# An attention and mixture block: the first LayerNorm by transposes instead of ones-vector sums, the expert gate ahead of the base GEMM, and weights loaded in rows

## The reference

```python
q = (x @ Wq.T).reshape(B, S, 16, 128)      # k, v likewise
scores = einsum('bshd,bsgd->bshg', q, k) / sqrt(128)   # heads of one token attend to each other
out = einsum('bshg,bsgd->bshd', softmax(scores), v).reshape(B, S, 2048)
x1 = layernorm(x + out @ Wo.T)
result = x1 @ base_w.T + base_b
probs = softmax(x1 @ router_w.T + router_b)
top_vals, top_idx = top_k(probs, 2)         # renormalised to a gate [token, 8]
mid = einsum('nd,edr->ner', x1, lora_A) * gate[:, :, None]
y = layernorm(x1 + result + 2.0 * einsum('ner,erd->nd', mid, lora_B))
```

## Time and profile before

| what | value |
|---|---|
| time, median of the runs shown | 2489.07 us (2457.67 and 2520.48) |
| profiled execution, device time | 2460.02 us |
| its span on the slowest core | 2458.4 us (other cores 2449.4 to 2455.0) |
| PE busy | 2221.6 us, 90% of the span |
| DVE, ACT busy | 1190.9 us (48%), 843.7 us (34%) |
| PE's granted clock, mean | 0.965 of full speed |
| HBM read, written | 180.70 MB, 8.39 MB |

### The profile page before, as it was taken

One profiled execution on the slowest core, in us unless ns is written; L12 is line 12 of the kernel. 1 busy time (PEld: TensorE's weight loads), 2 busy tenths in 40 slices (PEclk: granted clock), 3 DMA queues, 4 the chain that ended last, 5 costly groups with the idle time before them and its releaser, 6 DMA issues.

```text
span 2458.4 us, 32440 instructions; the slowest of 8 cores (2449.4 to 2458.4 us)
## 1 busy us (share of the span) xinstructions
PE 2221.6 (90%) x8920; PEld 1563.1 (64%) x8920; DVE 1190.9 (48%) x2085; ACT 843.7 (34%) x1514; POOL 12.6 (1%) x22
## 2 busy tenths in 40 slices
PE   6998999999899998899789999989998999888995
PEld 4666666666776651566566666666668666435664
DVE  2454444454654434544545445444447444255444
ACT  2333333333443420333333333333334343212333
POOL 0000000000000000000000000000000000000000
PEclk9999999999999998899889999999999999988997
DMA  4222222222112220222332222222220222111221
GB/s 138 86 78 78 86 86 86 78 78 86 36 58 82 78 78 7 79 78 82 142 112 84 84 82 79 85 78 86 81 83 19 79 78 80 58 43 61 78 86 78
DMA packets 50060, 191.19 MB, mean 78 GB/s; under 512 B 5632, under 2 KB 6048, under 8 KB 47584
## 3 DMA queue, kind: packets, MB, share of 16 engines
q1 hardware_dynamic: 47680, 176.38, 20.6%
q0 software_dynamic: 2208, 12.73, 1.5%
HBM read 180.70 MB, written 8.39 MB: 77 GB/s over the span
## 4 chain that ended last, share of the span: by engine, by line
PE 85%; DVE 6%; issue 5%; ACT 2%; DMA 1%; DVEq 0%; ACTq 0%; SPq 0%; POOL 0%; POOLq 0%
PE pb L238 29%; PE pb L245 23%; PE pb L254 23%; PE pb L771 1%; PE pb L764 1%; PE pb L678 1%; PE pb L688 1%; PE pb L371 1%; PE pb L423 1%; PE pb L861 1%; DVE xsp L213 1%; ACT xsp L210 1%; PE pb L407 1%; DMA wrawD<-wqT 1%; DVE bufC L328 1%
## 5 line engine op out<-in xcount | busy, mean ns | idle before, releaser
L238 PE MATMUL pb<-xsp,whi 128*128 128x512 f32 x2560 | 757.6, 418 | 137.1 <-DVE xsp L213 77.4
L238 PEld LDWEIGHTS pb<-xsp,whi 128*128 128x128 f32 x2560 | 439.4, 191 | 442.5 <-issue 383.0
L245 PE MATMUL pb<-xsp,whi 128*128 128x512 f32 x2560 | 700.6, 396 | 0.0
L254 PE MATMUL pb<-xsp,wlo 128*128 128x512 f32 x2560 | 694.1, 393 | 0.0
L245 PEld LDWEIGHTS pb<-xsp,whi 128*128 128x128 f32 x2560 | 487.8, 191 | 111.4
L254 PEld LDWEIGHTS pb<-xsp,wlo 128*128 128x128 f32 x2560 | 487.2, 190 | 107.8
L201 ACT CAST whi<-wrawD 128x512 fp32r<-128x512 f32 x320 | 198.4, 620 | 633.8 <-PE pb L254 601.9
L213 DVE TENSOR_TENSOR xsp<-xTs,xsp 128x512 fp32r<-128x512 f32 x384 | 265.5, 692 | 273.6 <-PE pb L245 273.6
L204 DVE TENSOR_TENSOR wlo<-wrawD,whi 128x512 fp32r<-128x512 f32 x320 | 221.3, 692 | 307.5 <-PE pb L238 234.8
L210 ACT CAST xsp<-xTs 128x512 fp32r<-128x512 f32 x384 | 236.7, 616 | 0.0
L201 ACT CAST whi<-bufA 128x512 fp32r<-128x512 f32 x128 | 79.4, 620 | 285.3 <-PE pb L254 285.3
(11 more groups left out here) (113 smaller groups left out, 888.5 us busy)
## 6 DMA issues: line engine op xcount, KB each, us to landing
wrawD<-wqT SPq DMA_DIRECT2D x32, 512.0 KB, 3.4
bufB<-wqT SPq DMA_DIRECT2D x32, 512.0 KB, 3.4
wrawD<-wkT SPq DMA_DIRECT2D x32, 512.0 KB, 3.3
avT<-wkT SPq DMA_DIRECT2D x32, 512.0 KB, 3.3
wrawD<-wvT SPq DMA_DIRECT2D x32, 512.0 KB, 3.2
avT<-wvT SPq DMA_DIRECT2D x32, 512.0 KB, 3.2
wrawD<-woT SPq DMA_DIRECT2D x32, 512.0 KB, 3.2
bufA<-woT SPq DMA_DIRECT2D x32, 512.0 KB, 3.2
```

Source lines behind the costliest of these rows:

```text
L238: e.matmul(pb[b][0:128, 0:T], whiB[wbi][:].bitcast(F32R)[:, j * 128:(j + 1) * 128], xhiB[wbi].bitcast(F32R), start=st, stop=False),
L245: e.matmul(pb[b][0:128, 0:T], whiB[wbi][:].bitcast(F32R)[:, j * 128:(j + 1) * 128], xloB[wbi].bitcast(F32R), start=False, stop=False),
L254: e.matmul(pb[b][0:128, 0:T], wloB[wbi][:].bitcast(F32R)[:, j * 128:(j + 1) * 128], xhiB[wbi].bitcast(F32R), start=False, stop=sp),
```

## The change

The five weights and the input stay plain two-dimensional arrays, and each transfer picks rows out of them: of a weight two runs of 2 KB for each partition, of the input four runs of 2 KB. The squares in the GEMM with Wo go. The first LayerNorm is done by `gen_ln` with its `back` part, in four chunks, with the two halves of `SH` as buffers. Router and lora A are two separate runs of 16 matmuls, and the whole gate stands between them and ahead of the base GEMM; `base_mid` keeps the last two DVE operations and is called at step 2. The small loads of the bias and of lora A wait for the end of the first LayerNorm.

```diff
-    d_wq = nc.dram_tensor("wqT", [D * D], F32, kind="ExternalInput").ap()
+    d_wq = nc.dram_tensor("wqT", [D, D], F32, kind="ExternalInput").ap()
...
                             emit("sync", lambda e, kc=kc, oc0=oc0, pair=pair:
-                                 e.dma_start(out=pair,
-                                             in_=wsrc(kc, oc0, 4)),
+                                 e.dma_start(
+                                     out=pair.rearrange("p (c e) -> p c e", c=2),
+                                     in_=wsrc(kc, oc0, 4, nkc=2)
+                                     .rearrange("(c p) e -> p c e", p=128)),
                                  waits=dw, inc=wsem, by=16)
...
-                        if q == 0 and ki == 8 and mid_cb is not None:
+                        if q == 0 and ki == 2 and mid_cb is not None:
                             mid_cb()
                         if ki == 2 and pending:
                             for fnp in pending:
                                 fnp()
                             pending = []
-                            if flush_cb is not None:
-                                flush_cb(q - 1)
...
-                for kq in range(4):
-                    off = (tile * 4 + kq) * 128 * 4 * T
-                    emit("sync", lambda e, kq=kq, off=off:
+                for kc in range(0, KC, 4):
+                    emit("sync", lambda e, kc=kc:
                          e.dma_start(
...
+                             in_=d_xT[kc * 128:(kc + 4) * 128, t0:t0 + T]
+                             .rearrange("(c p) t -> p c t", p=128)),
+                         waits=([x_free[0]] if kc == 0 else ()), inc="lx", by=16)
...
-                def wo_flush(qq):
-                    for oc in range(qq * 4, qq * 4 + 4):
-                        sq_se[oc] = emit("scalar", lambda e, oc=oc:
-                            e.activation(out=bufB[:, oc * T:(oc + 1) * T],
-                                         in_=xT[:, oc * T:(oc + 1) * T],
-                                         func=AF.Square),
-                            waits=[("dv", wo_ev[oc])], inc="se")
...
-                    lastsx = emit("tensor", lambda e, kc=kc:
-                        e.matmul(pb[0][0:1, 0:T], onesc[:],
-                                 xT[:, kc * T:(kc + 1) * T],
...
-                    sqmm[kc] = emit("tensor", lambda e, kc=kc:
-                        e.matmul(pb[1][0:1, 0:T], onesc[:],
-                                 bufB[:, kc * T:(kc + 1) * T],
...
-                        e.tensor_tensor(bufB[:, kc * T:(kc + 1) * T],
-                                        xT[:, kc * T:(kc + 1) * T],
-                                        pb[3][0:128, 0:T], op=ALU.mult),
...
+                x1n_dv = gen_ln(xT, bufB, src_ready=("dv", x1_dv))
+                x_free[0] = ("pe", cnt["pe"])
...
                 emit("gpsimd", lambda e: e.dma_start(
                      out=laT.rearrange("p (kc r) -> p kc r", r=128),
                      in_=d_la[:].rearrange("(kc p) r -> p kc r", p=128)),
-                     waits=[x1tok_free_g[1], ("dv", x1_dv)],
+                     waits=[x1tok_free_g[1], ("dv", x1n_dv)],
                      inc="la", by=16)
...
+                rw_w = [("lg", rw_ld), ("dv", x1n_dv), bank_free[rbank]]
                 for kc in range(KC):
-                    wr = [("dv", nrmB[kc])]
...
+                for c in range(NCH):
+                    t = GT2[c]
+                    lgt = emit("tensor", lambda e, c=c:
+                        e.matmul(pb[gbank][0:128, 0:8],
+                                 logT2[:, c * 128:(c + 1) * 128], i8[:],
+                                 is_transpose=True, start=True, stop=True),
+                        waits=[("dv", lge), bank_free[gbank]], inc="pe")
+                    lev = emit("vector", lambda e, t=t:
+                               e.tensor_copy(t["lgtok"], pb[gbank][0:128, 0:8]),
+                               waits=[("pe", lgt)], inc="dv")
+                    bank_free[gbank] = ("dv", lev)
...
+                la_w = [("la", la_ld), ("dv", x1n_dv), bank_free[labank]]
+                for kc in range(KC):
+                    lastm = emit("tensor", lambda e, kc=kc:
                         e.matmul(pb[labank][0:128, 0:T],
                                  laT[:, kc * 128:(kc + 1) * 128],
                                  bufB[:, kc * T:(kc + 1) * T],
...
+                    gxt_m[c] = emit("tensor", lambda e, c=c:
+                        e.matmul(pb[gbank][0:128, c * 128:(c + 1) * 128],
+                                 gexp2b[c], i128[:],
...
                 def base_mid():
-                    gate_chains()
...
                     emit("vector", lambda e:
                         e.tensor_copy(gateT2[:, 0:T], pb[gbank][0:128, 0:T]),
                         waits=[("pe", gxt_m[NCH - 1])], inc="dv")
```

More of the change, by code:

```diff
@@ L186, in stream_gemm @@
                         wcount[0] += 1
-                        pair = wrawD[:] if wri < 2 else w2ap
+                        pair = wrawD if wri < 2 else w2ap
                         wsem = wbuf_sem[wri // 2]
@@ L512, in program @@
                             w2ap=bufA[:, 0:1024],
[L513 to L514 removed]
+                            w2wait=[("pe", score1_pe[0])])
                 x1_dv = cnt["dv"]
@@ L671, in program @@
-                emit("vector", lambda e, onesr=onesr: e.memset(onesr, 1.0),
-                     waits=[("dv", x1_dv)], inc="dv")
-                lastsx = None
-                for kc in range(KC):
-                    w = [("dv", x1_dv), bank_free[0]] if kc == 0 else []
-                    lastsx = emit("tensor", lambda e, kc=kc:
-                        e.matmul(pb[0][0:1, 0:T], onesc[:],
-                                 xT[:, kc * T:(kc + 1) * T],
-                                 start=(kc == 0), stop=(kc == KC - 1)),
-                        waits=w, inc="pe")
@@ L682, in program @@
-                sqmm = {}
-                for kc in range(KC):
-                    w2 = [("se", sq_se[kc])]
-                    if kc == 0:
-                        w2.append(bank_free[1])
-                    sqmm[kc] = emit("tensor", lambda e, kc=kc:
-                        e.matmul(pb[1][0:1, 0:T], onesc[:],
-                                 bufB[:, kc * T:(kc + 1) * T],
-                                 start=(kc == 0), stop=(kc == KC - 1)),
-                        waits=w2, inc="pe")
@@ L707, in program @@
-                bank_free[1] = ("dv", var_dv)
-                sd_se = emit("scalar", lambda e:
-                    e.activation(out=rrow, in_=m2row, func=AF.Sqrt,
-                                 scale=1.0, bias=epsv[0:1, 0:1]),
-                    waits=[("dv", var_dv), ("dv", eps_dv)], inc="se")
-                emit("vector", lambda e: e.reciprocal(rrow, rrow),
-                     waits=[("se", sd_se)])
-                emit("vector", lambda e: e.drain())
-                mr_dv = emit("vector", lambda e:
-                    e.tensor_tensor(mrrow, murow, rrow, op=ALU.mult), inc="dv")
@@ L717, in program @@
-                rbc = emit("tensor", lambda e:
-                    e.matmul(pb[3][0:128, 0:T], onesr, rrow,
-                             start=True, stop=True),
-                    waits=[("dv", mr_dv), bank_free[3]], inc="pe")
-                emit("tensor", lambda e:
-                    e.matmul(pb[2][0:128, 0:T], onesr, mrrow,
-                             start=True, stop=True),
-                    waits=[bank_free[2]], inc="pe")
-                bc_pe = cnt["pe"]
-                nrmB = {}
@@ new lines, in program @@
+                bank_free[rbank] = ("dv", lge)
+                for c in range(NCH):
+                    t = GT2[c]
[8 more added lines that the diff above has]
+                    bank_free[gbank] = ("dv", lev)
+                    emit("vector", lambda e: e.drain())
+                    emit("vector", lambda e, t=t: e.reduce_max(t["m1"], t["lgtok"], axis=AX.X))
+                    emit("vector", lambda e: e.drain())
+                    emit("vector", lambda e, t=t: e.tensor_scalar(t["eq1"], t["lgtok"], t["m1"], None, op0=ALU.is_equal))
+                    emit("vector", lambda e: e.drain())
+                    emit("vector", lambda e, t=t: e.scalar_tensor_tensor(t["l2t"], t["eq1"], NEG_BIG, t["lgtok"], op0=ALU.mult, op1=ALU.add))
+                    emit("vector", lambda e: e.drain())
+                    emit("vector", lambda e, t=t: e.reduce_max(t["m2"], t["l2t"], axis=AX.X))
+                    emit("vector", lambda e: e.drain())
+                    g1 = emit("vector", lambda e, t=t: e.tensor_tensor(t["ddt"], t["m2"], t["m1"], op=ALU.subtract), inc="dv")
+                    emit("vector", lambda e, t=t: e.tensor_scalar(t["eq2"], t["lgtok"], t["m2"], None, op0=ALU.is_equal))
+                    ge_m[c] = emit("scalar", lambda e, t=t:
+                                   e.activation(out=t["e2t"], in_=t["ddt"], func=AF.Exp),
```

(11 more changed lines are left out.)

200 lines of the change are left out of this document (55 added, 145 removed).

## The result

The changed kernel takes 2435.9 us (median of 9 runs) beside 2460.8 for the kernel before (8 runs); the ratio of the two is 0.990, 95% interval 0.989 to 0.992. It is 24.9 us or 1.0% faster; 35.5 us had been forecast, and the range holds the time. (In some executions one die runs at a lower clock; these are left out of ratios, and medians are given where they are not touched by it.)

What follows compares the result with a forecast made beforehand. The prediction took PE's GEMM matmuls to bound the kernel. Per tile 3.4 - 13.5 - 8.4 = -18.5 us, two tiles -37.0, start +1.5: -35.5 from 2460.0, that is 2425 us, range 2406 to 2458.

Steps and rivals of the forecast that it cites:

- What bounds the kernel: Whole kernel: PE sets the end; work beside running GEMM steps is free, whatever stops a step or separates GEMMs is paid.
- Gate out of the base GEMM: Base GEMM, steps 7 to 9: moving the gate's small DVE operations out gives -13.5 us a tile, between -12.5 and -14.
- Squares: Wo GEMM, step 2 of quarters: without ACT's squares three flushes save 2.8 us each, -8.4 us a tile.
- Between the GEMMs: Wo GEMM to base GEMM: LayerNorm 44.5, router 15.5, then 0.2 and 20.5, together 80.7 us against 77.3, +3.4 a tile.
- Transfers: Weights and input in 2 KB runs: 0 in the GEMMs, +1.5 us at the start, where nothing covers them.
- the stretch: From the first PE instruction after the last addition into `xT` to the base GEMM: 80.7 us, +3.4 a tile.
- PE was at full clock in the router: Rival between the GEMMs: PE stays at half clock through router and lora A, +31.0 us a tile, 2480 us; chance 0.07.
- no weight was late: Rival in the GEMMs: weights in 2 KB runs land later than the 7.5 us allowed, 2505 us with e = 0.5; chance 0.05.
- the additions alone cost 0.6 a flush: Rival in the Wo GEMM: DVE's additions, not the squares, stop it; only the gate's part comes, 2442 us; chance 0.10.
- no 2% were gained: Rival for the whole: LayerNorm at full clock, no slow starts, a start that gains; 2408 us or a little under; chance 0.12.

Runs made afterwards that it cites:

- e3_gate8: Changed kernel with the gate's chains and transposes put back into the base GEMM at step 8: 2450.2 us, 14.3 above the changed kernel.
- e1_rows: Kernel before with only the changed kernel's row transfers of 2 KB: 2461.8 us, ratio to before 1.0003.
- e4_tiled: Changed kernel with the transfers of the kernel before: 2435.2 us, 0.7 below the changed kernel.
- e5_shift: Kernel before with the memset of `onesc` moved from the start into the first LayerNorm: ratio to before 1.001 (0.998 to 1.004).
- e6_memset: Changed kernel with the memset of `onesc` put back at the start: ratio to before 0.988 (0.981 to 0.995).
- e9_turn_at_once: Changed kernel with old transfers, memset back, router in four parts, lora A's weight loaded after attention, logits' transposes at once: 2397.3 us, ratio to before 0.9743.

## Why the prediction was right, and where it was off

- **What bounds the kernel** held: PE, and what stops it. But for the start and 2.9 us in the attention, the difference lies in steps that something stops and between the GEMMs.
- **Gate out of the base GEMM**, -13.5 a tile: measured -14.0 and -13.2, and +14.0 when it is put back.
- **Squares**, -8.4 a tile: -5.6 and -8.2 in the traces, and 14.0 in both tiles when they are put back. The mechanism was right (the wait on ACT's line 210 is gone); the size was off, since I took one flush for all three. By the steps the three flushes give 2.8, 2.9 and 1.5, which is 7.2 a tile: the 2.11 us wait costs 1.5 each time, the slow step behind it only sometimes. Four late starts of line 213 in the first tile's Wo GEMM take 1.4 of it away; that the second tile comes near the forecast is luck, since its first Wo step is 0.8 shorter (4.43 instead of 5.26), which no flush explains.
- **Between the GEMMs**, 80.7 us: measured 81.8. The parts: LayerNorm 46.2 for 44.5 (the clock was nearer to half than I took it; half gave 47), router 13.9 for 15.5 (its clock was full from its first matmul), lora A 4.9 behind the bias for 4.6, and 16.0 long for 15.4. That the errors of 1.7 and 1.6 in the first two cancel is luck. One sentence of it was wrong: "the gate in front costs nearly nothing, since it lies beside lora A". `e3_gate8` shows that it costs 7 us a tile, because lora A starts 3.6 later, and its first 3.5 us run at clock 0.50. The sum had those numbers in it, the sentence didn't.
- **Transfers**: 0 in the GEMMs and +1.5 at the start; measured 0 and +2.3 on core 0, +1.2 by the medians of the cores. The Trainium skill, "DMA: Bandwidth & Descriptors", Specifications, with line rate from 512 B on, would make it 0; the measurement shows a small cost at the start, where nothing hides it, which `e1_rows` and `e4_tiled` put at 0.9 to 1.0 us.
- **The step that failed** is the one never written down: that stages whose code is untouched keep their time. I had taken "in the GEMMs: 0" from the transfers alone. Against it stand +6.8 us: 4.2 for the 12 longer steps, caused by a memset that is no longer there (`e5_shift`, `e6_memset`), and 2.9 in the two attention stages (60.21 and 60.00 to 61.64 and 61.42), less 0.3 elsewhere. The attention varies from 58.6 to 63.0 us over cores and kernels with the same code, `e1_rows` with 61.94 among them, so core 0 alone says little. By the medians of the cores, though, the first tile's takes 59.3 to 59.7 in the eight profiled executions with the memset at the start and 60.8 to 61.2 in the six without it: there some 1.5 us go with the memset too. The second tile's shows no such split, and its cause stays open.

So -35.5 became -23.7: squares +3.0, the stretch +1.4, the start +0.8, the untouched stages +6.8, the base GEMM -0.2. The +0.8 of the start is particular to core 0. The forecast of 35.5 against a measured 24.9 got the direction, the stages and most of their prices; the range, 2406 to 2458, was so wide that it would have held a gain of 2 us or of 54, and the hit says little. None of the rivals came: PE was at full clock in the router, no weight was late, the additions alone cost 0.6 a flush, and no 2% were gained.

## What to carry to other kernels

Where an engine's wait stops a running GEMM, price the stop from several of its occurrences: the wait itself comes each time, the slow clock behind it only sometimes. A piece of serial work moved out of a GEMM to a place beside a long matmul run still costs what it delays that run's start, so look for what in it is needed first, and give that own columns or banks (as `e9_turn_at_once` does, together with an earlier load). And a change at the start of an engine's stream can move the time of unchanged code by some tenths of a per cent; before explaining a difference of 5 us in 2400, see at which steps it sits.

## What the runs showed of the hardware

- DVE has starts that are late by 0.34 to 0.41 us with no semaphore to blame, 128 records of its stream apart or a multiple of that (128 records are about 48 us of these GEMMs): all waits of PE for such a start, 136 over the eight cores of the changed kernel, fall on records 59 + 128 n, in every kernel here that has any. Whether it costs anything depends on which record stands there; one instruction more at the start of the program moves it. What happens there was not tried.
- A PE wait of 2.11 us was at some flushes followed by matmuls at a lower clock (steps of 4.1 to 4.5 us) and at others not, in the same kernel: in the kernel before the granted clock of the step behind was 0.66, 0.61 and 1.00 at the three flushes of the first tile.
- Router matmuls with 128 columns cost little more than a quarter of those with 512: four parts of 16 take 3.66 + 3.66 + 7.15 = 14.5 us, the whole 13.89.
